# Sixteen tiles through two transformer layers on one core: TensorE's transposes in the filled part done by VectorE in blocks and by DMA through DRAM

## What is computed

```python
# layer 0
h = rms(x) * (ln1_w * (1 + cond @ ln1_tw.T))           # per entry
q, k, v = h @ Wq.T, h @ Wk.T, h @ Wv.T                 # 8 heads of 64, one key and value head
attn = softmax(rope(q) @ rope(k).T / 8)                # within an entry: 64 x 64
x = x + (attn @ v) @ Wo.T
h = rms(x) * (ln2_w * (1 + cond @ ln2_tw.T))
x = x + (silu(h @ Wg.T) * (h @ Wu.T)) @ Wd.T           # 512 -> 2048 -> 512
# layer 1
h = layernorm(x) * (1 + scale) + shift                 # scale, shift from cond
q, c = h @ Wq.T, h @ Wkd.T                             # 16 heads of 32
k, v = c @ Wku.T, c @ Wvu.T                            # 4 key and value heads
out = x + (softmax(rope(q) @ rope(k).T / sqrt(32)) @ v) @ Wo.T
```

## Time and profile before

| | us |
|---|---|
| median of 3 runs | 899.96 (898.84 to 901.21) |
| profiled execution, first to last instruction | 898.5 |
| PE busy | 878.2 (98%) |
| DVE busy | 574.8 (64%) |
| ACT busy | 469.2 (52%) |
| POOL busy | 407.1 (45%) |
| DMA queue of SP | 72.07 MB, 23.3% of 16 engines' span |

### The profile page before, as it was taken

How to read it: one execution, slowest core, us unless ns; L and a number is a source line. 1 busy time by engine, 2 the same in 40 slices (tenths; PEclk the granted TensorE clock), 3 DMA queues, 4 the chain that set the end, 5 groups by cost and what they waited for, 6 DMA issues and landing times.

```text
span 898.5 us, 16045 instructions
## 1 busy us (share of the span) xinstructions
PE 878.2 (98%) x6172; PEld 735.6 (82%) x6172; DVE 574.8 (64%) x959; ACT 469.2 (52%) x861; POOL 407.1 (45%) x298
## 2 busy tenths in 40 slices
PE   8898999999999999999999999999999999999997
PEld 5687888888888888887887888888888888888885
DVE  6685556466556566557556676675765766758886
ACT  4665545445445455545537556455464464544662
POOL 1456545445435445446447554454443434431331
PEclk9899999999999999999999999999999999999999
DMA  9800322222222222222232222121222221200001
GB/s 345 331 25 24 118 83 82 71 82 83 71 82 83 71 82 71 70 73 87 71 117 71 71 71 68 56 95 53 83 83 71 83 82 57 76 12 13 25 25 36
DMA packets 31002, 73.18 MB, mean 81 GB/s; under 512 B 4304, under 2 KB 4816, under 8 KB 30928
## 3 DMA queue, kind: packets, MB, share of 16 engines
q1 hardware_dynamic: 30208, 72.07, 23.3%
q10 hardware_dynamic: 720, 0.09, 0.1%
HBM read 67.96 MB, written 4.19 MB: 80 GB/s over the span
## 4 chain that ended last, share of the span: by engine, by line
PE 87%; DVE 4%; issue 3%; ACT 2%; POOL 2%; DMA 0%; POOLq 0%; ACTq 0%; DVEq 0%
PE ps L486 26%; PE ps L488 25%; PE ps L487 25%; PE ps L591 2%; PE ps L764 1%; PE ps L571 1%; PE ps L532 1%; PE ps L742 1%; PE ps L752 1%; PE ps L578 1%; PE ps L718 1%; PE ps L621 1%; PE ps L691 1%; PE ps L556 1%; POOL qr L398 1%
## 5 line engine op out<-in xcount | busy, mean ns | idle before, releaser
L363 POOL TENSOR_TENSOR gul<-rgu,guh 128x1024 fp32r<-128x1024 f32 x64 | 156.5, 2445 | 187.9 <-ACT guh L1467 187.9
L1076 DVE TENSOR_TENSOR xres<-ps,xres 128x512 f32<-128x512 f32 x256 | 174.5, 687 | 88.1 <-PE ps L488 88.1
L486 PE MATMUL ps<-h2h,guh 128*128 128x512 f32 x512 | 205.8, 402 | 1.0 <-issue 1.0
L488 PE MATMUL ps<-h2l,guh 128*128 128x512 f32 x512 | 199.7, 390 | 0.0
L487 PE MATMUL ps<-h2h,gul 128*128 128x512 f32 x512 | 199.5, 390 | 0.0
L486 PEld LDWEIGHTS ps<-h2h,guh 128*128 128x128 f32 x512 | 96.2, 188 | 20.6 <-issue 1.4
L488 PEld LDWEIGHTS ps<-h2l,guh 128*128 128x128 f32 x512 | 96.1, 188 | 20.7
L487 PEld LDWEIGHTS ps<-h2h,gul 128*128 128x128 f32 x512 | 96.3, 188 | 18.6
L486 PE MATMUL ps<-wdh,ah 128*128 128x512 f32 x256 | 100.9, 394 | 1.2 <-DVE al L1071 1.2
L1489 ACT CAST ah<-af 128x512 fp32r<-128x512 f32 x64 | 39.7, 621 | 119.0 <-DVE af L1089 119.0
L488 PE MATMUL ps<-wdl,ah 128*128 128x512 f32 x256 | 99.8, 390 | 0.0
(11 more groups left out here) (172 smaller groups left out, 1690.3 us busy)
## 6 DMA issues: line engine op xcount, KB each, us to landing
rgu<-gu SPq DMA_DIRECT2D x64, 512.0 KB, 3.6
rwd<-WdT SPq DMA_DIRECT2D x64, 256.0 KB, 2.7
xt<-xT SPq DMA_DIRECT2D x16, 256.0 KB, 3.2
out<-xres SPq DMA_DIRECT2D x15, 256.0 KB, 3.0
xres<-x SPq DMA_DIRECT2D x1, 2560.0 KB, 13.4
adaw<-adaT SPq DMA_DIRECT2D x1, 2048.0 KB, 13.3
wst<-WqkvT SPq DMA_DIRECT2D x4, 320.0 KB, 6.1
adaw<-ln_twT SPq DMA_DIRECT2D x4, 256.0 KB, 4.0
```

Of the source, the lines that this page charges most:

```text
L363: pool.tensor_tensor(gul[i][:, :], rgu[i][:, :], guh[i][:, :], ALU.subtract).then_inc(m_gul, 1)
L486: pe.matmul(dst, lh, rh, start=start, stop=False)
L488: return pe.matmul(dst, lh, rl, start=False, stop=stop)
L1076: dve.tensor_tensor(at, bank(BD[i % 2]), at, ALU.add).then_inc(m_x, 1)
```

## The change

In the filled part VectorE turns tiles instead of TensorE. Its `transpose` turns blocks of 32 x 32 within a group of 32 partitions; `by_block` takes every fourth column for a block (512 columns are 4 x 4 x 32). The result is written to DRAM as it stands, one row for each partition (`away`), and read back with the pieces reordered (`back`: runs of 512 B for 512 columns and of 1 KB for 1024; `back_in_rows` for the queries and keys: 2560 runs of 128 B), so that it arrives in SBUF turned across all 128 partitions. Both transfers are issued by SP, in order with the loads of weights, and each waits on a semaphore. Moved are: the first layer's probabilities from step 5 on (`TURN_P0`), the tokens for the MLP from tile 4 on (`TURN_X2`), the second layer's tokens for tiles 0 to 10, its queries and keys for tiles 0 to 9, its probabilities for steps 0 to 8. The first layer's queries stay on TensorE (`TURN_Q0` is 16), and so does all from `TAIL` on. The consumers wait for the landing: `scores1` and `context`, `context1` on TensorE, `scale_h2` on VectorE (in two instructions now), `scale_shift_y` on ScalarE.

Some work moves with it. `scale_h2`, `high_h2` and `low_h2` of a moved tile stand behind the context of the step instead of ahead of its first fill. `load_group` is split into `load_gate_up` and `load_down`, placed by hand between the new transfers. In step 15 the load of `Wo1T` stands ahead of `y_back(0)`. The waits on banks that the turned tiles used are gone, and pT, pT1 and the context's casts have their columns in pieces of 32.

```diff
+TURN_P0, TURN_Q0, TURN_X2 = HEAD + 1, 16, HEAD
...
+        tq, tp = sb("tq", [P, D + P]), sb("tp", [P, 2 * D])
+        tx, ty = sb("tx", [P, D]), sb("ty", [P, D])
+        x2t, yt = sb("x2t", [P, W, KT, B32]), sb("yt", [P, W, KT, B32])
+        (dq0, dq1, dp0, dp1, dx, dy) = [
+            nc.dram_tensor("turned_" + n, [NT, P, cols], F32).ap()
+            for n, cols in (("q0", D + P), ("q1", D + P), ("p0", D), ("p1", 2 * D), ("x", D), ("y", D))]
...
+        def by_block(ap):
+            return ap.rearrange("p (k f q) -> p q k f", q=W, f=B32)
+        def turned(tile, cols):
+            return tile[:, 0:cols].rearrange("p (q k f) -> p q k f", q=W, f=B32)
+        def words(ap):
+            return ap.rearrange("p w k f -> p k w f")
+        def in_words(ap):
+            return ap.rearrange("p k (w f) -> p k w f", w=W)
...
-            def load_group(n):
-                g, i = n % NG, n % 2
-                wait(sp, m_gul, n - 1)
-                sp.dma_start(rgu[i][:, :], gu[g, :, :]).then_inc(ld_gu[i], 16)
-                wait(sp, m_wdl, n - 1)
-                sp.dma_start(rwd[i][:, :], WdT[g * P:(g + 1) * P, :]).then_inc(ld_wd[i], 16)
+            def load_gate_up(n):
+                if n < NN:
+                    wait(sp, m_gul, n - 1)
+                    sp.dma_start(rgu[n % 2][:, :], gu[n % NG, :, :]).then_inc(ld_gu[n % 2], 16)
+            def load_down(n):
+                if n < NN:
+                    g = n % NG
+                    wait(sp, m_wdl, n - 1)
+                    sp.dma_start(rwd[n % 2][:, :], WdT[g * P:(g + 1) * P, :]).then_inc(ld_wd[n % 2], 16)
+            def away(tile, to, cols, signal):
+                sp.dma_start(to, tile[:, 0:cols]).then_inc(signal, 16)
+            def back(tile, turn, signal):
+                sp.dma_start(tile[:, :, :, :].rearrange("p w k f -> p w (k f)"),
+                             turn.rearrange("(w f) (q c) -> (f q) w c", w=W, q=W)).then_inc(signal, 16)
+            def back_in_rows(tile, turn, signal):
+                sp.dma_start(tile[:, :, :].rearrange("p k (w f) -> p k w f", w=W),
+                             turn.rearrange("(w f) (q k c) -> (f q) k w c", w=W, q=W, c=B32)).then_inc(signal, 16)
...
+            def probs_away(t):
+                n = t - TURN_P0
+                sp.wait_ge(a_tp, n + 1)
+                away(tp, dp0[t, :, :], D, st_p0)
...
+                sp.wait_ge(st_p0, 16 * (n + 1))
+                sp.wait_ge(a_ctx, t)
+                back(pT, dp0[t, :, :], ld_p0)
...
+            def x2_back(t):
+                sp.wait_ge(st_x, 16 * (t - TURN_X2 + 1))
+                sp.wait_ge(a_gf, t)
+                back(x2t, dx[t, :, :], ld_x2T)
...
+            def y_back(t):
+                sp.wait_ge(st_y, 16 * (t + 1))
+                wait(sp, b_yf, t)
+                back(yt, dy[t, :, :], ld_yT)
...
+            n = 2
+            for s in range(HEAD, NT):
+                ready = PREP0.get(s)
                 if in_layer(s + 3):
                     load_xT(s + 3)
+                if s < TURN_P0:
+                    load_gate_up(n)
+                    continue
+                moved = ready is not None and ready >= TURN_X2
+                if moved:
+                    x2_away(ready)
+                load_down(n)
+                load_gate_up(n + 1)
+                probs_away(s)
+                if moved:
+                    x2_back(ready)
+                probs_back(s)
+                if TURN_Q0 <= s + 1 < NT:
+                    queries_away(s + 1)
+                    queries_back(s + 1)
+                load_down(n + 1)
+                load_gate_up(n + 2)
+                if s == NT - 1:
+                    y_away(0)
+                    sp.wait_ge(w1f, 1)
+                    sp.dma_start(w1st[:, :].rearrange("p (k n) -> p k n", k=KT), by_row(Wo1T)).then_inc(ld_w1, 16)
+                    y_back(0)
+                load_down(n + 2)
+                load_gate_up(n + 3)
+                n += 3
                 if s == NT - 2:
                     sp.wait_ge(w1l, 1)
                     sp.dma_start(w1st[:, 0:D], Wkd).then_inc(ld_w1, 16)
                     sp.dma_start(w1st[:, D:D + 2 * P], wkvuT).then_inc(ld_w1, 16)
+            for u in range(-1, NT):
+                ready = PREP1.get(u)
+                if ready is not None:
+                    x2_away(ready)
+                if u < TAIL:
+                    load_down(n)
+                    load_gate_up(n + 1)
+                    if ready is not None:
+                        x2_back(ready)
+                    if u >= 0:
+                        probs_away1(u)
+                        probs_back1(u)
+                    load_down(n + 1)
+                    load_gate_up(n + 2)
+                    y_away(u + 2)
+                    queries_away1(u + 1)
+                    y_back(u + 2)
+                    queries_back1(u + 1)
+                    load_down(n + 2)
+                    load_gate_up(n + 3)
+                    n += 3
+                if u > 0:
                     store(u - 1)
...
-                if s != HEAD + 1 and ready is not None:
+                if s <= HEAD and ready is not None:
...
+                if s > HEAD + 1 and ready is not None:
+                    low_h2(ready)
...
             def scores(t):
-                pe.wait_ge(a_qT, t + 1)
-                pe.wait_ge(a_kT, t + 1)
+                if t < TURN_Q0:
+                    pe.wait_ge(a_qT, t + 1)
+                    pe.wait_ge(a_kT, t + 1)
+                else:
+                    pe.wait_ge(ld_q0, 16 * (t - TURN_Q0 + 1))
...
-                p_T(s)
+                if s < TURN_P0:
+                    p_T(s)
...
-                if in_layer(s + 1):
+                if s + 1 < TURN_Q0:
                     qk_T(s + 1)
                 context(s)
-                if s == NT - 1:
-                    y_T(0)
...
-                if 0 <= u < NT - 1 and u != TAIL:
+                if TAIL < u < NT - 1:
                     p_T1(u)
                 fill(pieces, f3)
-                if in_layer(u + 1):
+                if u >= TAIL and in_layer(u + 1):
                     qk_T1(u + 1)
                 if 0 <= u < NT - 1:
                     context1(u)
-                if u < TAIL and in_layer(u + 2):
-                    y_T(u + 2)
                 fill(pieces, f4)
-                if u in PREP1:
-                    pe.wait_ge(a_ch, NT)
-                    pe.wait_ge(a_cl, NT)
-                    wait(pe, b_ch, u + 1)
-                    wait(pe, b_cl, u + 1)
-                    x2_T(PREP1[u], XB[2])
...
+            def turn_x2(t):
+                n = t - TURN_X2
+                dve.wait_ge(a_xn2, t + 1)
+                wait(dve, st_x, 16 * n)
+                dve.transpose(turned(tx, D), by_block(xn2[:, :])).then_inc(a_tx, 1)
...
+            def turn_probs(t):
+                n = t - TURN_P0
+                dve.wait_ge(a_p, t + 1)
+                wait(dve, st_p0, 16 * n)
+                dve.transpose(turned(tp, D), by_block(ex[:, :, :, :].rearrange("p j i s -> p (j i s)"))
+                              ).then_inc(a_tp, 1)
...
+            def turn_y(t):
+                dve.wait_ge(b_xn, t + 1)
+                wait(dve, st_y, 16 * t)
+                dve.transpose(turned(ty, D), by_block(yn[:, :])).then_inc(b_ty, 1)
...
+                moved = ready is not None and ready >= TURN_X2
+                if moved:
+                    turn_x2(ready)
...
+                if s >= TURN_P0:
+                    turn_probs(s)
...
+                if TURN_Q0 <= s + 1 < NT:
+                    turn_queries(s + 1)
+                if s == NT - 1:
+                    turn_y(0)
...
+                if moved:
+                    scale_h2(ready)
...
+                if 0 <= u < TAIL:
+                    turn_probs1(u)
...
+                if u < TAIL:
+                    turn_y(u + 2)
                 fill(pieces, f2)
-                if in_layer(u) and u != TAIL:
+                if u < TAIL:
+                    turn_queries1(u + 1)
...
             def scale_shift_y(t):
-                act.wait_ge(b_xT, t + 1)
                 wait(act, b_hl, t)
+                if t < TAIL + 2:
+                    act.wait_ge(ld_yT, 16 * (t + 1))
+                else:
+                    act.wait_ge(b_xT, t - TAIL - 1)
```

More of the change, by code:

```diff
@@ L54, in build @@
     QQ1, KK1 = D // 2, P // 2
+    B32 = P // W
     TWO_PI = 2 * np.pi
@@ L222, in y_bank1 @@
         def y_bank1(t):
-            if t == TAIL + 2:
-                return XB[1]
-            return banks1(t - 1)[3] if t - 2 >= TAIL else XB[3]
-        def preps_until(step, layer):
-            return sum(s <= step for s in PREP0) if layer == 0 else len(PREP0) + sum(u <= step for u in PREP1)
+            return XB[1] if t == TAIL + 2 else banks1(t - 1)[3]
         def w1_cols(w):
@@ L255, in store, with probs_away1, probs_back1 @@
+            def probs_away1(t):
+                sp.wait_ge(b_tp, t + 1)
```

(14 more changed lines are left out.)

284 lines of the change are left out of this document (174 added, 110 removed).

## The result

| | before | after |
|---|---|---|
| median, us | 899.99 (898.84 to 901.21, 4 runs) | 904.85 (902.72 to 905.10, 4 runs) |
| span of the profiled execution, us | 898.5 | 902.0 |
| ratio, 95% interval | | 1.0050 (1.0037 to 1.0063) |

A forecast was written before the change was run, and what follows sets the result against it. TensorE, an unbroken line of matmuls in the filled part, was taken to bound the kernel. 898.5 - 28.2 + 2.2 + 1.4 + 10.0 = 883.9 us of span, plus 1.5 for the runs' median: 885 us, range 872 to 900.

The forecast's parts named there:

- The gain: Both filled layers: 258 transposes taken off TensorE give back 28.2 us.
- The 0.59 of the earlier trace: Mid second-layer step: chain's figure for the tokens' four transposes; 0.15 taken as matmul-kind change that stays.
- VectorE's prices: VectorE's turns: 0.7 us for 512 columns, 0.8 for 640, 1.25 for 1024; ends 0.43 and 1.4 for 512.
- al becomes quick (0.69): First-layer step: with h2l moved behind both fills, al takes 0.69 not 1.36 and ends near 190.8.
- 0.2 lost in each of 11 steps: First-layer steps: al's cover is thin at 0.1 us, so 2.2 us lost in all; 0 to 9 possible.
- Step 14: Before the layer change: h2l and h2h ahead of the weights' split make al about 1.2 us later; loss 1.2.
- The two stops: Steps 15 and -1: y's late copy back delays al, so TensorE loses 4.1 and 3.7 us.
- 15 if each long stop also drops it: Layer change: the loss is 15 us, not 10.0, if long stops also lower the granted clock for a while.
- Steps 0 and 1: Start of second layer: step 0 gives 1.0 us of the gain back, ScalarE's line to al being as long as before.
- The queries' copy: Second-layer steps: 2560 runs of 128 B at 20 ns return in 5.0 us, hidden by 2.7 before the scores.
- Rival 3: Copies back through DRAM: moving part ten times slower, y 7 us too late in 11 tiles, above 962 us; chance 0.02.
- Rival 4: Late y each step: 1.0 us lost 9 times plus slow first-layer turns, 899; chance 0.06, half of that another 0.06.

The follow-up runs named there:

- late_turn: Changed kernel with y of tiles 0 to 2 and second-norm tokens of tiles 11 to 15 on TensorE, first-layer probabilities turned behind the first fill: 873.22 us.
- y_ahead: late_turn with y of tiles 0 to 2 on VectorE again, y's write-out and copy back ahead of the two weight loads on SyncE's queue: 875.13 us.
- sp_order: Changed kernel with only y's copy back issued right behind its writing out on SyncE's queue: 890.81 us, ratio 0.9907.
- x2_late: late_turn with second-norm tokens of tiles 12 to 15 on VectorE again, turned behind the second fill and the queries' turn: 875.71 us.

## Why the prediction was wrong

Its own ledger, by the stretches of the table. "Lost" is the time of after against the best that the same stretch showed in late_turn or y_ahead, less the transposes that these still have there:

| | lost, as predicted | lost, measured |
|---|---|---|
| first layer (A, B) | 2.2 | 1.1 + 5.0 |
| step 14 (C) | 1.2 | 3.5 |
| steps 15 and -1, start of 0 (D) | 4.1 + 3.7 + 1.0 | 12.9 |
| rest of step 0, step 1, start of 2 (E) | 0.3 | 9.6 |
| steps from 2 on (F) | 1.1 | 0.3 |
| sum | 13.6 | 32.4 |

1. **The gain** was right: 28.2 us forecast; 898.5 + 32.4 - 902.0 = 28.9 measured. Most of the difference is the second norm's tokens in the first layer, 0.57 for four and not 0.44, in eight steps; the prediction had no row of theirs. In a second-layer step the same four are worth 0.46 (36.18 against 35.72 in before). The 0.59 of the earlier trace rows is the second layer's tokens (line 691), and leaving 0.15 of it out was right: a steady step fell by 1.83, which is 0.87 + 0.55 + 0.41.
2. **VectorE's prices** were mis-sized by 1.5 to 1.6: 0.7, 0.8 and 1.25 against 1.09, 1.32 and 2.03. The prediction's rows read in plain order; the stride stands in the diff (by_block), and no row showed its price. The bounds held 1.09.
3. **First layer.** That al becomes quick (0.69) was right. Its end at 190.81 meets the forecast 190.8 only by luck, and TensorE wanted it at 190.33 and not at 190.9: the clock times of before were taken over, although after enters this step 0.63 us earlier by what it has gained. In the step's own time al was 0.6 late, 0.38 of it the longer turn. "0.2 lost in each of 11 steps" was 0.69 in six steps and 0.5 in two; and step 5, where turn and gf both stand ahead of h2h and h2l (TensorE's wait grew from 0.98 to 2.08 us), had no term. late_turn removes all of this.
4. **Step 14**: the mechanism as forecast, al beside the split of the weights, 3.5 us and not 1.2: the wait grew from 0.92 to 2.87, and the lower clock behind it cost 1.5 (416.73 to 421.23, 4.50 us; the same matmuls take 3.02 in before, from 417.93).
5. **The two stops** came where forecast, released by al, with yf waiting for the DMA: 5.07 and 4.00 us for 4.1 and 3.7. sp_order shows their cause. The clock's share, named there as "15 if each long stop also drops it", was left out of the sum. Matmuls at double distance cost some 1.8 us behind the first stop and 1.3 to 1.6 behind each of four others (2.87 in step 14, 4.00, 2.46 and 2.21), counted against the same row of matmuls at full clock: some 7.6 of the 32.4 us. D lost 12.9 for 8.8.
6. **Steps 0 and 1 are the step of the prediction that failed.** They were priced at 1.3 us and lost over 10 (the 1.55 at 504.8 is in D, and 2.46, 1.14 and 2.21 in E; some 3 us of E are the lower clock behind two of these). The prediction shows no timeline of VectorE for them. The turn of the second norm's tokens, ahead of af, and the scaling of gf from the copied tile had no term ("The x2 tile has more time still. Hidden", said of the first layer, is all there is). What stands ahead of the wait of 2.21, first in before, then in after (VectorE, GpSimd, TensorE):

```profile
552.83 0.67 DVE L1005 TENSOR_TENSOR gf<-ps,sc_ln 128x512 f32<-128x512 f32 x1
...
552.43 2.40 POOL L363 TENSOR_TENSOR gul<-rgu,guh 128x1024 fp32r<-128x1024 f32 x1 [0.68 <-ACT guh L1467]
```

```profile
566.30 2.35 DVE L1154 TENSOR_TENSOR gf<-x2t,sc_ln 128x256 f32<-128x256 f32 x2
...
573.68 1.09 DVE L1162 STREAM_TRANSPOSE tx<-xn 128x512 f32<-128x512 f32 x1
...
565.41 2.62 POOL L511 TENSOR_TENSOR gul<-rgu,guh 128x1024 fp32r<-128x1024 f32 x1 [0.19 <-ACT guh L1685]
...
577.90 0.61 PE L640 MATMUL ps<-wdh,ah 128*128 128x512 f32 x1 [2.21 <-DVE al L1244]
```

From the start of gf to that of af it is 7.48 us in before (552.83 to 560.31), 9.48 in after (566.30 to 575.78) and 8.49 in x2_late, which has the scaling but not the turn there (543.36 to 551.85): 1.0 is the turn and 1.0 the scaling, which beside the same gul takes 2.35 us from the copied tile and took 0.67 from the bank. The 2.46 has another cause: y, written out in 5.9 us behind weights, holds ScalarE for 3.49. By its mean VectorE is no fuller here than elsewhere, 0.74 and 0.78 of the two steps of E against 0.77 in a steady step that loses nothing; it is full in the ten microseconds around the scores (9.71 at 500, and in before 8.97 at 490). The runs split E's loss: putting y's copies in order gives back 3.35 of it, all of tiles 0 to 2 and 12 to 15 on TensorE gives 8.3 of it.
7. **Steady second layer**: right, 33.9 for a forecast 33.7, TensorE without gaps. The queries' copy: 3.7 us, so (3.7 - 1.8) / 160 = 12 ns a run for each DMA engine, an estimate by the prediction's fixed 1.8; the prediction took 20. Rival 3 (copies slower by ten) is refuted by the same row. Rival 4's late y holds ScalarE for 18.2 us in all, 14.3 of it in steps 15, -1 and 0 and 0.2 to 1.1 in each later one, and from step 1 on TensorE stops nowhere behind a late y.

The range of 872 to 900 was too narrow on the side where it erred: the sum took five places, each at a low value, and for a stretch never looked at it had no bound.

## What to carry to other kernels

Work that looks free by an engine's mean load is paid for at the places where that engine has no idle time. So when work moves to such an engine, read its timeline in the irregular steps too (start, change of stage), and not only in the steady one: here six second-layer steps gained 11 us, and the stretches D and E alone lost 22.5. Look as well at what reads the moved data: gf became slow because its source changed from a bank to SBUF. Keep moved work behind what the bounding engine waits for next (af and al here), even when it could run sooner. In a queue that issues in order, look at what each transfer stands behind, waits and bytes both: two moved lines were worth 14 us.

## What the runs showed of the hardware that I had not expected

- A VectorE transpose of f32 is as dear as a plain single-source operation (0.70 us for 512 columns) when it reads in order, and 1.5 times that (1.07 to 1.09) when it gathers every fourth word. A copy with the same stride takes 0.62.
- A copy by VectorE stretches beside GpSimd (1.12 to 2.80 us for 640 columns), as do the subtraction al (0.69 to 1.36, 3.5, 4.6) and the scaling of gf once it reads SBUF and not a bank (0.67 from the bank, 2.35 from SBUF, both beside GpSimd's gul). The transpose didn't in any of its ten turns of 640 columns (1.31 to 1.33).
- A 256 KB write to DRAM takes 2.0 us by itself and 5.3 to 6.0 issued right behind 768 KB of loads; 320 KB took 2.3, and 8.2 behind such loads and y's copies.
- Runs of 128 B cost some 12 ns each (the estimate above), yet the next issue on SyncE's queue behind the 2560 of them takes 1.6 to 2.2 us in after, up to 3.2 in y_ahead, and not 0.4.
- Behind TensorE's stops of 5.07 and 4.00 us the granted clock was at its lower level for some 3 to 4 us, and behind stops of 2.87, 2.46 and 2.21 us it fell too (0.50 from 418 to 420; 0.83 over the ten microseconds around each of the other two). Behind those of 1.55 and 1.14 it stayed at 1.00.
